# Attention and mixture-of-experts block on one core: products summed on TensorE, three input buffers, and new orders on every engine

## The reference, cut to what matters

```python
x                                   # (16, 56, 56, 32) float32: 16 images
# 1. windowed attention on layernorm(x)
xs = roll(ln(x), (-3, -3))          # 7x7 windows, 49 tokens each, 4 heads of 8
q, k, v = (xw @ w_qkv + b_qkv)      # per window
attn = softmax(q * scale @ k.T) + bias[None] + mask   # bias and mask are added behind the softmax
out  = (attn @ v) @ w_proj + b_proj
x    = x + roll_back(out)
# 2. mixture of experts on layernorm(x): 8 experts, the best 2 of each token
p    = softmax(t @ router_w + router_b)
top_p, top_i = top_k(p, 2);  top_p /= top_p.sum()
x    = x + sum_k top_p[k] * (t @ expert_w[top_i[k]] + expert_b[top_i[k]])
```

## Time and profile before

| | |
|---|---|
| three runs | 820.54, 822.0, 824.79 us; median 822.0 |
| the profiled execution | 823.93 us; its span in the trace 822.1 us |
| busy in the span | PE 603.0, PEld 406.6, DVE 585.8, ACT 370.9, POOL 355.3 us |
| instruction fetch | 97 packets on the queue "q8 instruction", 1.59 MB |
| DMA | 100.79 MB, mean 123 GB/s |

### The profile page before, as it was taken

The page is one execution under the profiler, slowest core; times in us unless marked ns, Lnnn a source line. Parts: engine busy times, 40 slices in busy tenths (PEclk is TensorE's granted clock), DMA queues, the critical chain, the costliest instruction groups (busy, mean ns, idle before and its releaser), DMA issues.

```text
span 822.1 us, 28813 instructions
## 1 busy us (share of the span) xinstructions
PE 603.0 (73%) x12210; PEld 406.6 (49%) x12210; DVE 585.8 (71%) x878; ACT 370.9 (45%) x737; POOL 355.3 (43%) x458
## 2 busy tenths in 40 slices
PE   2688788878687886777778787868787886886314
PEld 1456655545465554545545554645555555563101
DVE  7356768868787776878777787888788774766613
ACT  1565645454636435463644546463545434331100
POOL 2536463534536163453716454453737356123110
PEclk9999977979989688999989899998899798856555
DMA  4101338294755718384573938484665719175963
GB/s 112 35 4 42 71 99 185 57 197 100 160 125 112 171 50 200 94 184 101 129 153 76 197 75 199 101 182 100 144 139 127 176 45 199 41 169 120 203 149 81
DMA packets 40511, 100.79 MB, mean 123 GB/s; under 512 B 12736, under 2 KB 14784, under 8 KB 38848
## 3 DMA queue, kind: packets, MB, share of 16 engines
q1 hardware_dynamic: 39952, 98.05, 53.0%
q10 hardware_dynamic: 432, 0.90, 0.3%
HBM read 58.78 MB, written 8.03 MB: 81 GB/s over the span
## 4 chain that ended last, share of the span: by engine, by line
PE 48%; DVE 16%; ACT 12%; issue 12%; DMA 4%; POOL 4%; SPq 2%; ACTq 0%; POOLq 0%; DVEq 0%
PE ps_pv L1296 9%; PE ps_acc L1372 6%; PE ps_win L1278 5%; PE ps_win L1249 5%; DVE mx L979 4%; PE ps_shared L1213 4%; PE ps_shared L1228 3%; DMA gates<-shares_kept 3%; PE ps_shared L1316 3%; ACT pt L824 3%; PE ps_win L1257 3%; DVE gates L1082 2%; ACT mr L814 2%; ACT vb L781 2%; DVE st L969 2%
## 5 line engine op out<-in xcount | busy, mean ns | idle before, releaser
L979 DVE TENSOR_REDUCE mx<-ps_win 128x32 f32<-128x1568 f32 x64 | 114.5, 1789 | 90.5 <-PE ps_win L1249 90.4
L1082 DVE TENSOR_TENSOR gates<-gates,x 128x1792 f32<-128x1792 f32 x64 | 115.3, 1839 | 50.9 <-DMA gates<-shares_kept 50.3
L1296 PEld LDWEIGHTS ps_pv<-vb,pt 128*49 128x49 f32 x4096 | 113.2, 138 | 46.5 <-issue 42.3
L1296 PE MATMUL ps_pv<-vb,pt 128*49 128x18 f32 x4096 | 119.9, 207 | 19.4 <-issue 11.7
L640 POOL TENSOR_TENSOR on<-on,obs 128x256 f32<-128x256 f32 x64 | 46.5, 728 | 186.1 <-DVE on L1006 170.2
L824 ACT ACTIVATE pt<-ps_win 128x784 f32<-128x784 f32 x128 | 98.4, 821 | 51.7 <-PE ps_win L1278 51.7
L1278 PE MATMUL ps_win<-qbd,kp 32*49 32x196 f32 x2048 | 82.9, 376 | 12.8 <-issue 12.8
L1249 PE MATMUL ps_win<-kbd,qp 32*49 32x196 f32 x2048 | 65.5, 360 | 27.9 <-ACT pt L824 21.3
L814 ACT COPY mr<-ps_win 128x512 bf16<-128x512 bf16 x64 | 37.5, 586 | 104.0 <-PE ps_win L1257 103.9
L632 POOL TENSOR_SCALAR qbd<-qp,const_tile 128x392 f32<-128x392 f32 x128 | 78.5, 625 | 0.0
L606 POOL TENSOR_TENSOR xc<-xc,st 112x896 f32<-112x896 f32 x16 | 27.1, 1697 | 118.1 <-DVE st L948 118.1
(11 more groups left out here) (95 smaller groups left out, 1140.7 us busy)
## 6 DMA issues: line engine op xcount, KB each, us to landing
gates<-shares_kept SPq DMA_DIRECT2D x128, 392.0 KB, 10.0
x<-x SPq DMA_DIRECT2D x48, 392.0 KB
x_kept<-xin SPq DMA_DIRECT2D x16, 392.0 KB, 3.4
x<-x2t SPq DMA_DIRECT2D x64, 98.0 KB, 4.1
xin<-x SPq DMA_DIRECT2D x32, 150.0 KB
out<-xo SPq DMA_DIRECT2D x32, 150.0 KB
shares_kept<-shares SPq DMA_DIRECT2D x64, 24.5 KB, 1.5
xin<-x SPq DMA_DIRECT2D x32, 18.0 KB
```

Of the source, the lines that this page charges most:

```text
L979: nc.vector.tensor_reduce(mx[g % 2].rearrange("n a x h -> n a (x h)"), ps_win[:, :, 0:8 * N].rearrange("n a (k m) -> n a k m", m=N), AX, A ...
L1082: nc.vector.tensor_tensor(gate, gate, x4[w.par][:, :, columns(half)], ALU.mult).then_inc(gated, 1)
L1296: ins = mm(ps_pv[PAD * x:PAD * x + N, c0:c0 + SLOT], pt[g % 2][:, x, place, h, :], vb[u.par][:, 2 * g + x, a, h, :], start=True, stop=True)
```

## The change

It has seven parts. (1) The POOL sum `on + obs` goes. Instead of transposing the sum (4 transposes for each half of a unit), PE multiplies `on` with the identity and then `obs`, adding into the same PSUM range: 8 f32 products for each half. (2) The POOL sum x_kept + b_proj goes. Instead PE adds b_proj to the y product with one more f32 product for each half: a row of ones, as stationary operand of one row, times b_proj, repeated over 512 or 384 columns. (3) The second half of `kmask` goes from POOL to ACT. (4) Gate product 3 goes from DVE to POOL. (5) `keep` and `x_kept` go; there are three `xin` buffers, from which `back` reads, and a load waits for `y_added` of three units earlier. (6) `shares_kept` is laid out by expert, then block: a gates DMA now reads one run of 12,544 bytes for each partition instead of four of 3,136; its waits are for the low and the high half apart. (7) All order lists are new.

The core of the diff:

```diff
 STEPS = {
     "SP": [
-        ("store", 0, -3), ("replicate", 0, -1), ("keep", 0, 2), ("load", 0, 3), ("gates", 0, -1),
+        ("store", 0, -3), ("replicate", 0, -1), ("replicate", 1, -1), ("load", 0, 3), ("gates", 0, -1),
+        ("gates", 1, -1), ("gates", 2, -1),
     ],
...
-        shares_kept = nc.dram_tensor("shares_kept", (A * E, COLS), F32, kind="Internal").ap()
+        shares_kept = nc.dram_tensor("shares_kept", (E, A, COLS), F32, kind="Internal").ap()
...
             def load(v, _):
                 if v.has_before(1):
-
-                    sp.wait_ge(centered1, upto("centered1", v.before(1)))
-                    sp.wait_ge(x_kept_ready, upto("x_kept_ready", v.before(1)))
-                for tile, dram in pieces(x, xin, v):
+                    sp.wait_ge(x_loaded, upto("x_loaded", v.before(1)))
+                if v.has_before(INPUTS):
+
+                    sp.wait_ge(centered1, upto("centered1", v.before(INPUTS)))
+                    sp.wait_ge(y_added, upto("y_added", v.before(INPUTS)))
+                for tile, dram in pieces(x, xin[v.number % INPUTS], v):
                     sp.dma_start(tile, dram).then_inc(x_loaded, 16)
 
-            def keep(v, _):
-                sp.wait_ge(x_loaded, upto("x_loaded", v))
-
-                if v.has_before(2):
-                    sp.wait_ge(y_added, upto("y_added", v.before(2)))
-                sp.dma_start(x_kept[v.par].rearrange("p j k c -> p (j k c)"),
-                             xin.rearrange("p j k c -> p (j k c)")).then_inc(x_kept_ready, 16)
...
+                    for b in range(4):
+                        rows = bass.AP(shares_kept.tensor, shares_kept.offset + BLOCK * b,
+                                       [[COLS, A], [A * COLS, E], [1, BLOCK]])
+                        sp.dma_start(rows, shares[32 * b:32 * b + 32, :]).then_inc(shares_stored, 16)
...
+                    sp.wait_ge(mixed, upto("mixed", w.before(1), 2 + eh))
+                for e in range(4):
+                    row = bass.AP(shares_kept.tensor, shares_kept.offset + (4 * eh + e) * A * COLS,
+                                  [[0, C], [1, A * COLS]])
...
-            def pv(u, g):
-
-                pool.wait_ge(pv_drained, upto("pv_drained", u, g))
-                pool.wait_ge(ob_drained, upto("ob_drained", u))
-                o = on[:, g, :, :].rearrange("p k r -> p (k r)")
-                nc.gpsimd.tensor_tensor(o, o, obs[u.par][:, g, :, :, :, :].rearrange("p k a h d -> p (k a h d)"),
-                                        ALU.add).then_inc(o_ready, 1)
...
+            def mul(w, _):
+
+                pool.wait_ge(x4_ready, upto("x4_ready", w))
+                pool.wait_ge(gates_high, upto("gates_high", w))
+                gate = gates[:, 1, :, columns(1)]
+                nc.gpsimd.tensor_tensor(gate, gate, x4[w.par][:, :, columns(1)], ALU.mult).then_inc(gated_pool, 1)
...
             def ot_turn(u, i):
 
                 shared_free("ot", u, i)
-                pe.wait_ge(o_ready, upto("o_ready", u, 2 * i + 1))
+                pe.wait_ge(pv_drained, upto("pv_drained", u, 2 * i + 1))
+                pe.wait_ge(ob_drained, upto("ob_drained", u))
                 turned = shared("ot", u, i)[:, :].rearrange("p (g x k m) -> p g k x m", g=2, x=2, k=2)
                 for g in range(2):
                     for k in range(2):
-                        ins = nc.tensor.transpose(turned[:, g, k, :, :], on[:, 2 * i + g, k, :], ident[:, :])
+                        mm(turned[:, g, k, :, :], on[:, 2 * i + g, k, :], ident[:, :], start=True, stop=False,
+                           skip_group_check=True)
+                        ins = mm(turned[:, g, k, :, :], obs[u.par][:, 2 * i + g, k, :, :, :].rearrange("p a h d -> p (a h d)"),
+                                 ident[:, :], start=False, stop=True, skip_group_check=True)
                 ins.then_inc(ot_filled, 1)
...
-                for k in range(*((0, 4) if i == 0 else (4, 7))):
+                k0, k1 = (0, 4) if i == 0 else (4, 7)
+                mm(bank[0:ROWS, 0:128 * (k1 - k0)], one_row[:, :], bp.unsqueeze(1).to_broadcast([1, A * (k1 - k0), C]),
+                   start=True, stop=False, skip_group_check=True)
+                for k in range(k0, k1):
```

More of the change, by code:

```diff
@@ L67 @@
 GAP_STEP = 9
+INPUTS = 3
 LEFT = 4 * ROWS
@@ L118 @@
+        ("mul", 1, -3), ("maximum", 0, 0), ("mul", 2, -3), ("pv", 3, -1), ("top2", 0, -2), ("top2", 1, -2),
+        ("top2", 2, -2), ("norm1_root", 0, 1), ("place", 0, 2), ("final", 0, -3), ("maximum", 1, 0),
+        ("final", 1, -3), ("top2", 3, -2), ("top2", 4, -2), ("back", 0, -1), ("back", 1, -1),
+        ("norm2_center", 0, -1), ("pv", 0, 0), ("maximum", 2, 0), ("norm2_scale", 0, -1), ("norm1_center", 0, 2),
+        ("pv", 1, 0),
     ],
     "PE": [
-        ("route", 0, -2), ("pv", 3, -1), ("logits", 0, -2), ("sum", 0, -3), ("shift", 0, 0), ("ot", 0, -1),
@@ L126 @@
-        ("maximum", 0, 1),
+        ("ot", 0, -1), ("scores", 0, 0), ("ob", 0, 0), ("sum", 1, -3), ("ot", 1, -1), ("maximum", 1, 0),
+        ("final", 0, -3), ("sum", 2, -3), ("sum", 3, -3), ("pv", 0, 0), ("final", 1, -3), ("y", 0, -1), ("y", 1, -1),
+        ("shift", 1, 0), ("xt", 0, 1), ("scores", 1, 0), ("share", 0, -2), ("ob", 1, 0), ("maximum", 2, 0),
[3 rows of a table added]
+        ("shift", 0, 1),
     ],
@@ L164 @@
     ],
     "PE": [
-        ("route", 13, 0), ("logits", 13, 0), ("ob", 15, 0), ("shift", 15, 0), ("ot", 14, 0), ("pv", 14, 3),
-        ("scores", 15, 0), ("sum", 12, 0), ("maximum", 15, 1), ("sum", 12, 1), ("sum", 12, 2), ("ot", 14, 1),
-        ("final", 12, 0), ("sum", 12, 3), ("pv", 15, 0), ("shift", 15, 1), ("y", 14, 0), ("scores", 15, 1),
-        ("final", 12, 1), ("maximum", 15, 2), ("y", 14, 1), ("share", 13, 0), ("shift", 15, 2), ("scores", 15, 2),
-        ("pv", 15, 1), ("maximum", 15, 3), ("pv", 15, 2), ("x2t", 14, 0), ("x2t", 14, 1), ("shift", 15, 3),
@@ L176 @@
-        ("sum", 15, 3), ("final", 15, 0), ("final", 15, 1),
+        ("ob", 15, 0), ("scores", 15, 0), ("ot", 14, 0), ("sum", 12, 1), ("ot", 14, 1), ("sum", 12, 2),
+        ("maximum", 15, 1), ("sum", 12, 3), ("pv", 15, 0), ("final", 12, 0), ("shift", 15, 1), ("y", 14, 0),
+        ("final", 12, 1), ("scores", 15, 1), ("share", 13, 0), ("y", 14, 1), ("maximum", 15, 2), ("ob", 15, 1),
+        ("pv", 15, 1), ("shift", 15, 2), ("scores", 15, 2), ("maximum", 15, 3), ("x2t", 14, 0), ("x2t", 14, 1),
@@ new lines @@
+        ("pv", 15, 2), ("shift", 15, 3), ("sum", 13, 0), ("scores", 15, 3), ("route", 14, 0), ("logits", 14, 0),
+        ("pv", 15, 3), ("sum", 13, 1), ("ot", 15, 0), ("sum", 13, 2), ("ot", 15, 1), ("final", 13, 0),
+        ("sum", 13, 3), ("share", 14, 0), ("final", 13, 1), ("y", 15, 0), ("y", 15, 1), ("x2t", 15, 0),
+        ("x2t", 15, 1), ("route", 15, 0), ("logits", 15, 0), ("sum", 14, 0), ("sum", 14, 1), ("final", 14, 0),
+        ("share", 15, 0), ("sum", 14, 2), ("sum", 14, 3), ("final", 14, 1), ("sum", 15, 0), ("sum", 15, 1),
@@ L177 @@
+        ("sum", 15, 2), ("sum", 15, 3), ("final", 15, 0), ("final", 15, 1),
     ],
@@ L701, in _ @@
                     place(unit, i)
[L702 to L705 removed]
+                elif step == "mul" and i == 3:
+                    mul(unit, i)
                 elif step == "top2" and i == 5:
@@ L895, in _ @@
                     k_drain(unit, i)
-                elif step == "kmask" and i == 0:
+                elif step == "kmask":
                     kmask(unit, i)
```

190 lines of the change are left out of this document (79 added, 111 removed), and 30 rows, old and new, of tables (LAST, STEPS).

## The result

Four runs of the changed kernel gave 830.38 to 844.54 us, median 833.93; the kernel before, beside it, 821.27. The ratio is 1.0136, 95% interval 1.0072 to 1.0200: **slower**, by some 1.4%, where 811 was forecast (786 to 838). The ratio leaves out slow runs such as the 844.54 here; the trace of the kernel before (823.93) is itself of a slow one, but at the clock of the trace after (0.854 against 0.853). Here are views of the profiled execution (835.91 us, span 834.1).

A forecast was written before the change was run, and what follows sets the result against it. PE was taken to bound the period by work, lost clock and short waits, with gates barely on time. Period 46.56 to 45.0, twelve times: 823.9 - 19 + 8 for the ends = 813, 811 us at the runs' median; range 786 to 838.

The forecast's parts named there:

- PE's new work: On PE, ot as products instead of transposes and the row of ones for y: +4.6 us a unit (3.7 to 5.0).
- B: PE's stretch from sum 0 to the end of the next y: 20.9 us plus 1.5 for gaps, 22.4.
- A: PE's stretch from the end of y to sum 0: 22.6 us after the change, from 33.33.
- the lost clock: Time PE loses to the lower clock level: 5.1 us a period before, expected to shrink with the waiting.
- c: The clock loss left in PE's stretch from y to sum 0 after the change: forecast 2.7 us.
- the lost clock stays: Slower rival, PE between y and sum 0: clock loss stays at 5.0 us, period 47.3, time 839; chance 0.22.
- the gaps on "issue": Gaps inside PE's matmul runs, 38.5 us in all before; the slower rival said they start the lower clock.
- the first units: The start, where PE has work while nothing else waits: forecast +2 us.
- tail: Last stretch at a clock of 0.53, with the last unit's ot and y on the path: forecast +6 us.
- Gates: The way from the end of y through the gates' DMA to the end of product 0: forecast 22.0 us.
- Product 3: Gate product moved from DVE to POOL: 0 us forecast, bounds 0 and 1 us a period in the middle.
- Long rows: Longer runs in the gates' DMA reads: forecast to give nothing for the gates.

The follow-up runs named there:

- the swap: Third pv put ahead of the first half of x2t in PE's list, against the changed kernel: 828.97 us, ratio 1.0131 to the kernel before.
- the kernel with both back: The changed kernel with both sums (on + obs, and b_proj) on POOL again, all else as changed: 802.39 us, ratio 0.9838 to the kernel before.

## Why the prediction was wrong, point by point

- **PE's new work** was priced right: forecast 4.6 us a unit, measured 2 x 1.93 - 1.18 + 1.86 = 4.5. An f32 product takes 0.24 against a transpose's 0.148, 1.6 times as long. The Trainium skill (TensorE: Matmul & The Clock Gate, Terms) has a factor of four there; by these two durations it does not hold in this kernel.
- **B** came to 22.6, with 22.4 forecast, but by errors that cancel: its work was 20.4 instead of 20.9 and its waiting 1.1 instead of 1.5, and it lost 1.2 to the lower clock, which the prediction had put at nothing from one period. **A's** work was right (15.2 against 15.0); its waiting was right in size alone (4.7 against 4.5), as 1.5 of it is the new wait at x2t.
- **The step that failed in the periods is the lost clock**: "if the loss goes with the waiting (about 5 now), c is 2.7". Waiting fell as forecast and the loss stayed: c = 4.1 in A, and 5.3 in the whole period, as before (5.1). The sum had left out B's 1.5 of gaps, too; with 6.2 of waiting its own rule gives 5.1 x 6.2 / 9.4 = 3.4. The rule itself does not hold: the kernel with the swap and both sums on POOL waits 9.2 us a period and loses 3.7. The rival "the lost clock stays", said to decide from 3.6 on, is what came, but mostly by another cause than the one given there: the gaps on "issue" became fewer (10 over 0.75 us, 23 us in all, instead of 18 and 38.5), and a new wait came. In four traces of kernels with the new orders and the swap, c is 1.3 to 2.8 and the loss of the whole period 3.4 to 3.7; in nine without the swap they are 3.7 to 6.2 and 4.5 to 7.0 (those with the load moved left aside). With the swap alone the gaps on "issue" are about the same, 9 of them, 20 us in all. I had counted x2t among what fills other steps' waits, and not asked when its own data come. In all, the periods and units 13 and 14 gained 7 us where 19 were forecast, a miss of 12.
- **The second step that failed, as large as the first, is the first units**: +2 forecast, 14.9 measured, 2.5 of it only because of what now stands ahead of y. I took the work of two units as mostly hidden. PE does wait there, for 37 us, but the new work fills next to none of it: the sums cost 12.3 in this pair of traces and 9 over all of them. That is a miss of 13. The **tail** came to 4.1 instead of 6, which is luck: the 6 were for the sums, and the kernel with both back has no shorter tail (70.7 against 69.9); in the old orders they add 2.2 there (67.9 against 65.7).
- The span closes with the four stretches: 822.1 + 14.9 (first units) - 3.7 (11 periods) - 3.3 (units 13 and 14) + 4.1 (end) = 834.1.
- **Gates** at 22.0 after y: where sum 0 waits for them, A is 22.6. **Product 3** at no cost in the middle: nothing shows there; in the last unit product 2 takes 2.5 us longer, where I had put 0. **Long rows** at nothing: nothing shows.

So the change is two things: new lists and a copy less, worth 17 us, and two sums on PE that cost more than that, 24 by the ratios. That the time came near the rival's 839 is luck as well: the period is 46.2 and not its 47.3, and the first units bring the rest.

## What to carry to other kernels

Work given to the busiest engine hides only in waits that it can fill: here about two thirds of it in the steady part, and next to nothing in the first units, although the engine waits there too. When a list is laid out anew, ask of each step that moves when its own data come, and what else its engine could do until then. If an edit removes one wait and moves no time, look where the wait went (here to two other steps, and the lost clock in part to the next stretch), and try both cures together.

## What was not expected of the hardware

Moving one 1.5 us wait, which came behind one of 0.8, out of a stretch took 2.8 us of lost clock a period out of that stretch; 1.3 came back in the next one. The lost clock does not go with the sum of the waits: 5.3 us a period with 5.6 of waiting, 3.7 with 9.2. A product with one row of contraction costs as much as products with 112 rows: 1.03 us for 512 columns, against 1.06 for four of 128. Rows of 12,544 instead of 3,136 bytes, 25,410 packets instead of 38,466, change no time that shows. One load, moved behind the gates' DMAs, made a reader wait 19.8 us and cost 200 us in all.
